# A fused post-norm block on one core: norm 3, branch, logits and gap of the last batch reordered around the weight folds; generators by three transfers, identity products at the front

## The reference, cut to what matters

```
x = layernorm(x + attn(x))           # 8 batches x 512 tokens x 256
x = layernorm(x + ffn(x))
# attn: norm1, gates, selective scan, out projection, norm2, MLP (gelu), residual
# ffn:
xn = layernorm(x) * ln_gamma + ln_beta
abel_out = gelu(xn @ abel_w + abel_b)              # "branch"
logits = xn @ moe_gate_w + moe_gate_b              # 8 experts
topw, topi = top_k(logits, 2); topw = softmax(topw)
moe_out = sum over the two experts of w * (gelu(xn @ ew1[e] + eb1[e]) @ ew2[e] + eb2[e])
for i in range(3):
    moe_out = moe_out @ expm(gens[i])
gate = sigmoid([abel_out, moe_out] @ gc_w + gc_b)
return x + abel_out * (1 - gate) + moe_out * gate
```

## Time and profile before

| | |
|---|---|
| runs | 717.41, 717.82, 718.45 us |
| profiled execution | 717.39 us |
| its span (first to last instruction) | 715.6 us |
| PE busy | 664.6 us (93%) |
| DVE busy | 580.4 us (81%) |
| ACT, POOL busy | 459.2, 247.2 us |

### The profile page before, as it was taken

How to read it: one execution, slowest core, us unless ns; L and a number is a source line. 1 busy time by engine, 2 the same in 40 slices (tenths; PEclk the granted TensorE clock), 3 DMA queues, 4 the chain that set the end, 5 groups by cost and what they waited for, 6 DMA issues and landing times. The chain is left out here.

```text
span 715.6 us, 16536 instructions
## 1 busy us (share of the span) xinstructions
PE 664.6 (93%) x4673; PEld 504.2 (70%) x4700; DVE 580.4 (81%) x1538; ACT 459.2 (64%) x860; POOL 247.2 (35%) x307
## 2 busy tenths in 40 slices
PE   5899999999999999999999987999999999999890
PEld 5667657566575856657575876778888888887770
DVE  5989768899898999989899977587777877775484
ACT  4246483865749486574948454678877778775175
POOL 2102030034618153361806443043434334343153
PEclk9899999999999999999999999899999999999996
DMA  5643214156553735455764834377666545610794
GB/s 148 205 147 59 89 27 92 60 89 222 114 148 94 163 106 104 163 114 143 236 145 146 250 126 127 59 176 161 158 172 161 153 110 155 151 44 20 247 313 147
DMA packets 124535, 99.22 MB, mean 139 GB/s; under 512 B 60464, under 2 KB 114619, under 8 KB 124348
## 3 DMA queue, kind: packets, MB, share of 16 engines
q1 hardware_dynamic: 108060, 68.82, 33.9%
q0 software_dynamic: 16416, 29.67, 17.6%
HBM read 62.42 MB, written 33.68 MB: 134 GB/s over the span
## 5 line engine op out<-in xcount | busy, mean ns | idle before, releaser
L1984 POOL DMA_INDIRECT scratch_ys<-ye,place x78 | 80.7, 1034 | 147.2 <-ACT ye L2037 108.0
L79 PE MATMUL banks<-shared,words 128*128 128x256 bf16 x936 | 110.3, 275 | 5.7 <-PEq L1762 5.7
L79 PE MATMUL banks<-words,shared 128*128 x936 | 110.4, 274 | 1.8 <-issue 0.8
L79 PE MATMUL bank<-words 128*128 128x512 bf16 (+1 forms) x567 | 107.6, 343 | 4.3 <-DVE logits L1089 3.2
L79 PEld LDWEIGHTS banks<-shared,words 128*128 x936 | 92.2, 99 | 18.1 <-issue 6.4
L79 PEld LDWEIGHTS banks<-words,shared 128*128 128x128 bf16 x936 | 90.6, 98 | 16.4 <-issue 3.9
L79 PEld LDWEIGHTS bank<-words 128*128 128x128 bf16 x576 | 55.5, 98 | 50.4 <-issue 6.6
L79 PE MATMUL bank<-mlp_w,shared 128*128 128x256 bf16 x768 | 86.5, 273 | 0.0
L79 PE MATMUL bank<-xn_s,mlp_w 128*128 128x512 bf16 x368 | 83.7, 379 | 1.5 <-DVE xn_s L810 0.7
L520 POOL DMA_INDIRECT scratch_zs<-rows,pos x64 | 71.2, 1112 | 35.2 <-issue 17.0
L79 PEld LDWEIGHTS bank<-mlp_w,shared 128*128 128x128 bf16 x768 | 75.0, 98 | 10.6 <-issue 0.4
(11 more groups left out here) (259 smaller groups left out, 1222.9 us busy)
## 6 DMA issues: line engine op xcount, KB each, us to landing
fetched<-scratch_zs SPq DMA_DIRECT2D x156, 64.0 KB
words<-scratch_ys SPq DMA_DIRECT2D x14, 514.0 KB, 8.6
scratch_abel<-staged SPq DMA_DIRECT2D x8, 514.0 KB, 3.5
abel_all<-scratch_abel SPq DMA_DIRECT2D x8, 514.0 KB, 5.7
x_in<-in_x SPq DMA_DIRECT2D x8, 512.0 KB, 5.2
words<-in_out_b_row SPq DMA_DIRECT2D x8, 512.0 KB, 4.0
fetched<-in_mlp_b_row SPq DMA_DIRECT2D x8, 512.0 KB, 3.7
words<-in_x POOLq DMA_DIRECT2D x8, 512.0 KB, 7.9
```

Source lines behind the costliest of these rows:

```text
L79: last = nc.tensor.matmul(dst, lhs(a, k), rhs(b, k), start=start and n == 0, stop=stop and n == total - 1)
L1984: nc.gpsimd.indirect_dma_start(out=ys_dram[:, :], out_offset=bass.IndirectOffsetOnAxis(ap=place[:, k, s:s + 1], axis=0), in_=ye[:, k % 2, ...
```

## The change

Generators: one transfer of 768 KB becomes three of 256 KB with a semaphore each, so that PE can turn the first matrix when the first has landed; DVE still waits for all three. PE gets ten identity products (128 columns, fp32, bank 3) before the first turn and fourteen after `turn1(0)`.

Last batch: the orders of PE, DVE and ACT are rewritten, `rstd3` goes behind the third instead of the fourth send of batch 6, `logit_rows` waits for the branch (`ab_done`) and no longer for the gelus, the gelus wait for the logits, `ranks` uses bank 5 instead of bank 3, and PE waits for `pos_r` before it reuses that bank (fold 14).

```diff
-            sp.dma_start(A, t["gens"].rearrange("g (k p) n -> p g k n", p=P)).then_inc(gens_in, 16)
+            for s in range(GENS):
+                sp.dma_start(A[:, s], t["gens"][s].rearrange("(k p) n -> p k n", p=P)).then_inc(gens_in[s], 16)
...
-                    if r == 0:
-                        rest()
+                        if r == 0 and n == after - 1:
+                            rest()
...
-            send(LAST - 1, lambda: rstd3(LAST))
+            send(LAST - 1, lambda: rstd3(LAST), TT - 1)
...
-            w2_heads(range(FC, 3 * FC))
+            w2_heads(range(FC, 2 * FC + 2))
             z4_heads(LAST)
-            w2_heads((3 * FC, 3 * FC + 1))
+            w2_heads((2 * FC + 2,))
+            nc.scalar.preload_act_table_set("natural_log_exp_and_others")
+            w2_heads((2 * FC + 3,))
+            gap_exps(LAST)
             nc.scalar.preload_act_table_set("gelu_and_others")
+            act.wait_ge(lg_r, 2 * TT * BATCHES)
             branch_gelus(LAST)
-            nc.scalar.preload_act_table_set("natural_log_exp_and_others")
-            w2_heads((3 * FC + 2,))
-            gap_exps(LAST)
-            w2_heads(range(3 * FC + 3, NE * FC))
-            nc.scalar.preload_act_table_set("gelu_and_others")
+            w2_heads(range(3 * FC, NE * FC))
...
-            w1_tails((5, 6))
+            w1_tails((5,))
             branch_sum(LAST, LAST % 2, 0)
-            w1_tails((7,))
+            dve.wait_ge(v_r, 2 * LAST + 1)
+            stats_of(v, st3, st3_r, (0, 1))
             branch_sum(LAST, LAST % 2, 1)
-            norm3(LAST)
+            dve.wait_ge(v_r, 2 * LAST + 2)
+            stats_of(v, st3, st3_r, (2, 3))
+            spreads_of(st3, st3_r, mv3, mv3_r, LAST)
+            norm3_spreads(LAST)
             w2_tails(range(FC, 2 * FC))
             norm3_rows(LAST)
-            w2_tails(range(2 * FC, 3 * FC))
+            w1_tails((6,))
+            w2_tails((2 * FC, 2 * FC + 1))
             z4_tails(LAST)
-            w2_tails((3 * FC, 3 * FC + 1))
-            logit_rows(LAST)
+            w1_tails((7,))
+            w2_tails((2 * FC + 2,))
+            logit_rows(LAST, ab_done)
             picked_of(LAST)
-            w2_tails((3 * FC + 2,))
             count_on(LAST)
             weigh(LAST)
             places(LAST)
-            w2_tails((3 * FC + 3,))
+            w2_tails((2 * FC + 3,))
...
-            w2_tails(range(4 * FC, 5 * FC))
+            w2_tails(range(3 * FC, 4 * FC))
...
-            w2_tails((5 * FC, 5 * FC + 1))
+            w2_tails((4 * FC, 4 * FC + 1))
...
-            w2_tails(range(5 * FC + 2, 6 * FC))
+            w2_tails(range(4 * FC + 2, 6 * FC))
...
                 if j == LAST:
-                    pe.wait_ge(gelu_r, TT * BATCHES)
+                    pe.wait_ge(w2_tail, 2 * FC + 3)
...
+                    elif m in (16, 17):
+                        pe.wait_ge(gelu_r, TT * LAST + m - 13)
...
+            def busy(n):
+
+                for _ in range(n):
+                    nc.tensor.matmul(bank[3][:, 0:P], ident[:, :], ident[:, :], start=True, stop=True)
...
+            busy(10)
             round_turns(0, A)
             round_products(0, A)
             round_turns(GENS, A2)
             turn1(0)
+            busy(14)
             round_products(GENS, U, True)
...
             fold(1)
-            fold(2)
+            fold(2, (0, 1))
             turn4(LAST, BATCHES + 1)
+            fold(2, (2,))
+            branch(LAST, BATCHES + 1)
+            fold(2, (3,))
             fold(3, (0, 1))
-            branch(LAST, BATCHES + 1)
+            ranks(LAST)
+            pe.wait_ge(pos_r, BATCHES)
             fold(3, (2,))
-            ranks(LAST)
-            fold(3, (3,))
             pe.wait_ge(seen_r, BATCHES)
+            pe.wait_ge(gelu_r, TT * LAST + 1)
             nc.tensor.matmul(bank[2][:, 0:NE], ones[:, :], seen[:, BATCHES % 2, :], start=True, stop=True)\
                 .then_inc(cnt_done, 1)
+            fold(3, (3,))
```

More of the change, by code:

```diff
@@ L323, in branch_bank, with rank_bank @@
             return bank[(2, 3, 6, 7)[n] if j == LAST else n]
+        def rank_bank(j):
+            return bank[5 if j == LAST else 4]
         def turn_banks(j):
@@ L504, in add_x1, with send @@
                 nc.gpsimd.dma_start(x_res[:, par], x1[:, :, :], accum_op=ALU.add).then_inc(xres_r, 16)
-            def send(j, rest=lambda: None):
+            def send(j, rest=lambda: None, after=TT):
                 if j == 0:
@@ L796, in stats, with stats_of, spreads_of @@
             def stats(src, st, st_r, mv, mv_r, b):
-                for n in range(TT):
+                stats_of(src, st, st_r, range(TT))
+                spreads_of(st, st_r, mv, mv_r, b)
+            def stats_of(src, st, st_r, ns):
+                for n in ns:
                     nc.vector.bn_stats(st[:, n], src[:, n]).then_inc(st_r, 1)
+            def spreads_of(st, st_r, mv, mv_r, b):
                 dve.wait_ge(st_r, TT * b + TT)
@@ L849, in square_copy @@
                 nc.vector.tensor_copy(A2[:, s], mat(3 + s)).then_inc(mat_r, 1)
-            dve.wait_ge(gens_in, 16)
+            for s in range(GENS):
+                dve.wait_ge(gens_in[s], 16)
             absolute_rows(A, 0)
```

17 lines of the change are left out of this document (10 added, 7 removed).

## The result

The changed kernel takes 715.35 us in the median of seven runs, the kernel before 717.7 beside it: a ratio of 0.996, with a 95% interval of 0.9948 to 0.9972. It is faster by 0.28 to 0.52%, where 710.2 us and a range of 708.5 to 713.8 had been forecast: the sign is right, the time is 5 us off and outside the range. The profiled execution took 714.74 us, with a span of 713.0 (before 715.6).

What follows compares the result with a forecast made beforehand. PE (93% busy) and DVE (81%) hand a chain back and forth, neither alone the bound. 717.39 - 2.75 (front) - 3.15 (last batch) - 1.95 (phase B's clock) = 709.55, stated as 710.2 us, range 708.5 to 713.8.

Steps and rivals of the forecast that it cites:

- (c) to (f): Last batch: norm 3, branch and logits earlier, `pos_r` 3.15 us earlier; later folds nearly tie and cost nothing.
- (a): Front: ten identity products raise the clock, the turns take about 1.47 us, and DVE's copy comes 0.85 us earlier.
- (b): Front: fourteen identity products keep the clock up, `U` starts at 19.7, its products take 5.5 us; front total -2.75 us.
- (g): Start of phase B: PE idles only 2.3 us, the clock stays up, and the first tiles gain 1.95 us.
- The sum: Whole kernel: front -2.75, last batch -3.15 and phase B's clock -1.95 us, all carried to the end: 709.55.
- front hidden: Rival, 15%: ten products end late or fourteen don't keep the clock; front gives 0.85 or less; 712.1 us, or 714.0.

Runs made afterwards that it cites:

- Last only: The changed kernel with the front of the kernel before (one transfer, no identity products at the front): 713.87 us, ratio 0.9953.
- three only: The kernel before with the generators in three transfers, nothing else: 717.59 us, ratio 1.0002.
- one, longer: The changed kernel with one transfer of the generators and 21 identity products behind the first turn, not 14: 714.60 us, ratio 0.9964.
- one transfer: The changed kernel with the generators in one transfer again, identity products kept: 713.84 us, ratio 0.9962.
- third fetched: The changed kernel with three tiles fetched ahead of the barrier of phase B, not two: 713.45 us, ratio 0.9952.
- identities only: The kernel before with the ten and fourteen identity products, generators in one transfer: 716.50 us, ratio 0.9989.
- none before tiles: The changed kernel without the nine identity products ahead of phase B: 714.42 us, ratio 0.9963.
- single covers: Changed kernel with either 21 identity products after the first turn (715.59 us, 0.9969) or two ahead of the last ranks (715.25 us, 0.9965).
- both in place: Changed kernel with one transfer, 21 identity products after the first turn and two before the last ranks: 712.49 us, 0.9934; third tile fetched too: 711.96 us, 0.9925.
- after: The changed kernel itself, against the kernel before: 715.35 us, ratio 0.9960.
- rank cover: The changed kernel with two identity products ahead of the ranks of the last batch: 715.25 us, ratio 0.9965.
- front only: The kernel before with the front of the change (three transfers and both groups of identity products): 719.14 us, ratio 1.0016.
- third group: Four variants of the changed kernel: 21 identity products after the first turn, or POOL's first power moved to DVE: ratios 0.9969, 0.9964, 0.9957, 0.9948.
- all of the second: Four variants of the changed kernel: one transfer, an early all-reduce added, no products before phase B, third tile fetched: ratios 0.9962, 1.0088, 0.9963, 0.9952.
- library early: The changed kernel with one transfer and a small unread all-reduce on POOL ahead of the first power: 723.20 us, ratio 1.0088.

## Why the prediction was wrong

**The last batch, (c) to (f): right.** Rows 4.3 us behind the end of `mlp_down` (forecast 4.3), `pos` 15.1 (15.4), phase B 39.0 (38.8), the stall at fold 24 1.01 us (1), folds done at 438.9 (439.1). From 41.9 to 39.0 are 2.9 us of the 3.15 forecast. The first branch gelu started at 420.93, 0.02 us behind its table load, and cost the chain nothing. *Last only* alone gives 0.9953.

**Step (a) failed first: "Three transfers carry the same bytes; DVE and norm 1 still need all of them."** From that I took that DVE starts when it did. It starts 1.1 us later in the changed kernel and 1.0 later in *three only*, and nothing uses the first matrix earlier, since the ten products end at 6.54. These ran at the low level to their end, the upper bound of (a), so the turns took 2.30 us and not 1.47.

**Step (b) failed by it.** PE's products on `U` were to start at 19.7, 0.85 earlier than before; they started at 21.22, 0.7 later. The pause ahead of its products was not 1 us but 1.89, and "so it should stay" was not true at 1.89, though it had been at 2.23. I had treated the longest pause without a fall as a bound. There is none to be read from one row: in these profiles the clock fell over 1.89, 2.08 and 2.27 us ahead of `U` and stayed over 1.62, 1.84, 2.07 and 2.21; ahead of phase B it fell over 2.67 (*one, longer*) and stayed over 3.15 (*one transfer*) and 3.56 (*third fetched*). What the front is worth with the clock up, 2.75, was right at the end of `mlp_down` (2.8 in *identities only*).

(b) also left a link out: POOL. DVE's wait for the all-reduce was not in my reading. In the kernel before, POOL's power ends at 10.88, the all-reduce goes at 16.85 and DVE starts `U` at 19.63. With the turns faster and the generators as early as before (*identities only*) DVE has its sum ready at 15.93 in place of 16.72, 0.8 us earlier as (a) said, but POOL, 5.72 us behind its power, goes at 16.59 and `U` starts at 19.38: 0.25 us gained and not 0.85. The rest of the 2.8 came behind `U`, from the clock.

**Step (g) was right in what it named and wrong in its price.** PE idled 2.50 us (2.3 forecast), the clock stayed up, and the first two tiles' products took 5.50 us. "In the first tiles nothing else stands in the way: PE was working in all of that time" was the error: a slow PE is busy all the time because it is slow. From the start of phase B to the fifth tile's second products are 30.4 us before and 30.1 after. PE waits 0.49, 0.98, 0.22 and 0.87 us in these tiles, DVE 1.73, 2.55 and 2.16 for fetched rows. The term of 1.95 measured 0.2; *none before tiles*, at the low level there, has 29.8.

**The sum.** -0.28 for -2.75, -2.9 for -3.15, and +0.6 for -1.95 from phase B's start to the end. The first five tiles still gain 0.2; the loss lies behind them, 0.4 us up to the thirteenth tile and 0.3 more up to the 38th, and why wasn't tried. (Added up again, the prediction's sum is 709.54 and, with its 0.43, 709.97, for 709.55 and 709.95.)

**What (a) and (b) don't explain.** The sum took every us of the front to the end. Even with the clock up that is not so: in *one transfer* the front is 2.7 us ahead of the changed kernel's at the end of `mlp_down`, 1.3 at the start of phase B, 1.1 at the fifth tile and nothing at the tenth, and by the medians it adds nothing to *last only*. So a front as forecast would have reached `mlp_down` and still not have given 2.75 us in the median.

**The rivals.** The case that came true stood there in part: *front hidden*, "the clock isn't kept by the fourteen", at 15% and with 712.1. Its time was wrong since it rested on (g); without (g) the prediction has 714.0 for it.

**What stays open.** Why the third and fourth logit copies come late in every profile with `pos` at 15.7, though PE's rows stand at the same distance. How often the clock falls in executions without a profile: that falls in some of them spoil single covers fits the medians, but is argued, not measured, and by the marks above a fall costs little. And *one transfer*, whose clock stayed up throughout, still starts phase B 1.4 us later behind `mlp_down` than the changed kernel; 0.6 is that copy, and the rest comes with the eight transfers that fetch the first two tiles (SP, changed kernel and then *one transfer*), of which the second tile's land late:

```profile
435.11 4.57 SPq L52 DMA_DIRECT2D fetched<-scratch_zs  x8
```

```profile
432.90 5.70 SPq L52 DMA_DIRECT2D fetched<-scratch_zs  x8
```

They take 4.5 to 4.6 us in ten of the profiles and 5.5 to 5.9 in five; what makes them longer is open.

## What to carry to other kernels

When an engine's speed depends on its pauses, list its pauses from start to end, short ones in a row too: one cover showed nothing here, and with both in place 1.9 to 2.5 us came out by the ratios, of which the clock explains only a part. Follow a gain to the end before you add it to a sum, stage by stage in the same profile: here it shrank at the start of phase B and again at a single late transfer. Compare a profile's own time with the median before you read one from the other. Price a faster engine by who feeds it, since an engine at half speed looks fully busy and hides the waits that its speed will uncover. And splitting a transfer helps only a reader of the first piece; here the one engine that needed the last piece set the pace.

## What the runs showed of the hardware

- The same pause does not do the same: 1.89 us dropped the clock in one profile, and 2.21, 2.50, 3.15 and 3.56 kept it in others; *after* and *rank cover*, whose fronts hold the same instructions, differ in it over 1.89 and 2.07 us, and the same 2.23 us kept it in the kernel before and dropped it in *front only* and *three only*. Nor does the rise come at the same place: the ten identity products at the start took 3.90 us in *front only*, 4.32 in *one transfer* and 4.63 in *after*. The Trainium skill (TensorE: Matmul & The Clock Gate, Part 1: The HAM clock gate) says that the number of slow matmuls varies from run to run; these three lengths agree.
- Two short pauses, 0.66 and 1.41 us with some tiny matmuls between, dropped the clock in four profiles and not in four others; 0.17 to 0.19 and 1.41 in none of four. The four falls are all of the third group and the four others all of the second, on another chip, so the chip may have a part in it; the covers ran on the chip of the falls.
- GpSimd needed 5.5 to 7.8 us between an all-reduce and its elementwise arithmetic or `iota`, in both directions, with nothing to wait for that the profile shows (5.54 after the power in the changed kernel; 7.82 and 7.00 behind an all-reduce in *library early*).
- The 768 KB of the generators let DVE start at 5.7 to 6.5 as one transfer and at 6.7 to 7.2 as three.
